# Attention outputs gathered by channel with DMA, and projected without transposes

## The chip, the cores and the metric

The kernel runs on one core of a Trainium2 chip. The metric is device time in microseconds, median of several runs. Engines: PE (TensorE, matrix products), ACT (ScalarE), DVE (VectorE), POOL (GpSimd), and SP (SyncE), whose sequencer here issues every DMA.

## What is computed

```
xn = layernorm(x)                        # x: 8 batches, 1024 tokens, 256 channels, float32
Q, K, V = xn wq^T, xn wk^T, xn wv^T      # 16 heads of 16 channels; rotary embedding on Q and K
attn = softmax(causal(Q K^T / 4)) V      # per head
s = attn wo^T
g = silu(down(silu(gate(xn)) * up(xn)))  # weights are int32, scaled by 1/127
out = x + s * g
```

## The kernel before

It has two phases. `project_phase` writes q, k, v and the gate g to DRAM; `attention_phase` begins at about 400 us. Float32 accuracy is had by splitting operands into a high and a low float16 part.

The attention phase runs over 8 batches of 4 **groups**; a group is four heads of one batch (a `step` is (batch, group)). All engines run the same group loop, each in its own written order, and meet at semaphores.

A group has 36 **turns** on PE, set by the string `ORDER`. An E turn makes one of 18 units of keys-by-queries scores (L1363), from which ACT makes exponentials (`pr`, L1281). An M turn makes one of 18 units of queries-by-keys scores (L794, with the causal mask added by products with `future` and `pick`, L802), of which DVE takes the maximum (L818). These maxima are for later groups: a group takes maxima 7 to 17 of the next group and 0 to 6 of the one after it. Turn t writes two PSUM banks, slot t mod 3, and waits in `wait_slot` until the unit of turn t-3 has been consumed, by ACT if that was an E turn, by DVE if it was an M turn.

Between turns PE runs whole-array blocks at places given by numbers: ten products with v (`times_v`, L1380, `V_AT`; places of 36 and above fall in the next group), a transpose of the joined maxima (L833, `MAXT`), and the work on finished outputs. Product s=0 waits until ACT has copied the second half of the group before out of its bank (`take_output`, L1288, `TAKE1`), product s=3 until it has copied the first half of this group (`TAKE0`).

Outputs of a group come out of `times_v` with channels on partitions: per head 16 rows of output, one row of sums (v is extended with a column of ones, the rest zero) and 15 rows of zeros. ACT copies each half (512 queries) to `ot`, PE transposes it (`transpose_output`, L1394, four 128x128 float32 per half, `OUT1`, `OUT0`), ACT copies it to `on` (L1293), DVE inverts the 16 sums of a row (L1171, `NORM1`, `NORM0`), POOL multiplies into `an` (L1109). When the four groups of a batch are done, its eight tiles of 128 tokens are projected, two in each later group (`output_tiles`): POOL splits a tile (L1099, L1101, `HALVE`), PE transposes the parts (`transpose_tile`, L1402, `TR`), ACT copies them to `aT` (L1298), PE multiplies by wo (`project_tile`, L1410, `WO`), ACT copies the product to `ws` (L1304, `MUL`), POOL multiplies by the gate and adds x (`ADD`). The first batch's four groups have no tiles to project, so no L1402 and no L1410 runs in them. The last group and the four tiles after it have orders of their own (`last_group`, `end_tiles`).

The maxima of the next group are transposed, negated on DVE (L840, `NEG`), split on POOL (L849, L851) and stored by SP as rows of `qs` (`load_max`, L861); the first E turn of the next group waits for that. SP's queue per group is: 8 loads of q and k (L775 to L778), one of v, tile loads and stores in some groups, and the 4 of `load_max`.

## Time and profile before

| | us |
|---|---|
| median of 3 runs | 1221.46 (1220.7 to 1222.96) |
| profiled execution | 1220.83 |
| its span | 1219.1 |

Busy shares of the span: PE 96%, DVE 80%, ACT 72%, POOL 52%. The second phase is a nearly periodic run of groups, each between 24.4 and 25.1 us long, so a change of one group counts some thirty times. A busy time is the union of modelled spans; what an instruction occupies is better read from one start to the next.

### The profile page before, as it was taken

What the parts mean: (1) busy time and instruction counts of PE and PEld (TensorE: products, weight loads), DVE (VectorE), ACT (ScalarE), POOL (GpSimd) and SP (SyncE); (2) the same over time, 40 slices, a digit from 0 to 9 for tenths busy, and PEclk for the clock granted to TensorE, in tenths of its full rate; (3) what the DMA queues carried; (4) which work ended last, traced back from release to release, by engine and by line L of the source; (5) the groups of instructions that cost most, each with busy time, mean ns of one, the idle gap of its engine ahead of it and who ended that gap; (6) DMA issues with size and microseconds to landing.
All of it is one profiled execution on the core that took longest, in us unless ns stands there. A gap on an engine that the chain in (4) does not pass through costs nothing.

```text
span 1219.1 us, 29979 instructions
## 1 busy us (share of the span) xinstructions
PE 1176.2 (96%) x10707; PEld 554.8 (46%) x10707; DVE 971.1 (80%) x1160; ACT 880.6 (72%) x1123; POOL 638.2 (52%) x996
## 2 busy tenths in 40 slices
PE   5999999999999889999999999999999999999997
PEld 3565556656555333334444443444444444444333
DVE  6666666667777689988898899889888988898843
ACT  4554554454444588788888888888888888888884
POOL 5765665765564322444455445554565455445554
PEclk9999999999999899999999999999999999999998
DMA  9755454566642511332323313333144133332122
GB/s 254 191 173 155 141 187 135 157 191 172 167 136 87 147 45 46 98 79 72 97 76 110 97 46 106 73 103 97 49 122 113 45 98 88 97 97 58 59 71 88
DMA packets 157888, 134.81 MB, mean 111 GB/s; under 512 B 49472, under 2 KB 142144, under 8 KB 157760
## 3 DMA queue, kind: packets, MB, share of 16 engines
q1 hardware_dynamic: 157760, 133.08, 38.7%
q8 instruction: 83, 1.36, 0.5%
q14 instruction: 45, 0.37, 0.1%
HBM read 72.61 MB, written 50.33 MB: 101 GB/s over the span
## 4 chain that ended last, share of the span: by engine, by line
PE 61%; ACT 2%; DVE 1%; issue 1%; POOL 1%; ACTq 0%; DVEq 0%; POOLq 0%
PE ps L1380 23%; PE ps L1363 14%; PE ps L794 12%; PE ps L1410 4%; PE ps L802 3%; PE ps L1394 3%; PE ps L1402 2%; ACT pr L1281 1%; DVE mxp L818 1%; PE ps L833 1%; ACT on L1293 0%; POOL ah L1101 0%; POOL zt L1119 0%; DVE yt L1219 0%; ACT ot L1288 0%
## 5 line engine op out<-in xcount | busy, mean ns | idle before, releaser
L818 DVE TENSOR_REDUCE mxp<-ps 128x2 f32<-128x1024 f32 (+2 forms) x576 | 685.3, 1221 | 91.0 <-PE ps L802 50.6
L1281 ACT ACTIVATE pr<-ps 128x1024 f32<-128x1024 f32 x576 | 575.8, 1023 | 100.5 <-PE ps L1363 86.1
L1380 PE MATMUL ps<-pr,vt 128*32 128x512 f32 (+3 forms) x3072 | 315.3, 497 | 0.6 <-POOL pr L1091 0.5
L1363 PE MATMUL ps<-qs,ks 50*128 50x512 f16 (+3 forms) x1536 | 225.6, 329 | 8.6 <-DVE mxp L818 4.2
L794 PE MATMUL ps<-ks,qs 48*128 48x512 f16 (+2 forms) x1792 | 225.2, 304 | 8.2 <-ACT pr L1281 4.8
L1091 POOL TENSOR_SCALAR_AFFINE_SELECT pr<-pr 128x256 f32<-128x256 f32 (+1 forms) x448 | 191.6, 454 | 51.3 <-ACT pr L1281 51.0
L1363 PEld LDWEIGHTS ps<-qs,ks 50*128 50x128 f16 x1536 | 65.4, 93 | 212.7 <-issue 201.6
L674 PE MATMUL ps<-xTh,wguT 128*128 128x512 f16 x384 | 145.8, 380 | 1.2 <-ACT vs L558 1.1
L674 PE MATMUL ps<-xTl,wguT 128*128 128x512 f16 x384 | 145.5, 379 | 0.0
L794 PEld LDWEIGHTS ps<-ks,qs 48*128 48x128 f16 x1792 | 83.0, 94 | 98.6 <-issue 85.0
L849 POOL TENSOR_SCALAR mp<-mneg 32x128 f16<-32x128 f32 x32 | 9.3, 289 | 206.3 <-issue 200.9
L1380 PEld LDWEIGHTS ps<-pr,vt 128*32 128x32 f32 x3072 | 67.3, 108 | 104.4 <-issue 94.7
L433 DVE SCALAR_TENSOR_TENSOR h<-ps,sg 128x512 f32<-128x512 f32 x96 | 65.8, 686 | 48.6 <-ACT sg L566 36.9
L552 ACT ACTIVATE parts<-rr 128x1024 f16<-128x1024 f32 x32 | 33.8, 1057 | 77.8 <-POOL rr L500 77.6
L566 ACT ACTIVATE sg<-ps 128x512 f32<-128x512 f32 x96 | 57.1, 595 | 43.5 <-PE ps L674 23.6
L802 PE MATMUL ps<-future,pick 64*128 64x128 bf16 (+3 forms) x1024 | 85.7, 242 | 0.0
L648 PE MATMUL ps<-xTh,wqkT 128*128 128x512 f16 x256 | 80.4, 384 | 4.4 <-DVE wqkT L383 4.4
L361 POOL TENSOR_TENSOR hl<-h,hh 128x512 f16<-128x512 f32 x64 | 72.8, 1159 | 22.2 <-ACT hh L572 22.2
L424 DVE TENSOR_TENSOR rot<-ps,trig 128x1024 f32<-128x1024 f32 x64 | 75.3, 1219 | 7.5 <-PE ps L648 7.1
L1127 POOL TENSOR_TENSOR yt<-ws,gt 128x256 f32<-128x256 f32 x53 | 38.6, 729 | 76.3 <-ACT ws L1304 76.3
L500 POOL TENSOR_TENSOR rr<-rot 128x1024 f32<-128x1024 f32 x32 | 74.9, 2361 | 5.8 <-DVE rot L424 5.8
L1109 POOL TENSOR_TENSOR an<-on,rec 128x256 f32<-128x256 f32 x61 | 37.9, 622 | 60.6 <-DVE rec L1171 60.6
(104 smaller groups left out, 1355.9 us busy)
## 6 DMA issues: line engine op xcount, KB each, us to landing
v_d<-vs SPq DMA_DIRECT2D x16, 1024.0 KB, 5.3
vt<-v_d SPq DMA_DIRECT2D x32, 512.0 KB, 4.0
xs<-in_L_attn_x SPq DMA_DIRECT2D x16, 512.0 KB, 4.5
q_parts_d<-parts SPq DMA_DIRECT2D x16, 512.0 KB, 3.0
k_parts_d<-parts SPq DMA_DIRECT2D x16, 512.0 KB, 3.1
gate_d<-gs SPq DMA_DIRECT2D x16, 512.0 KB, 3.2
qs<-q_parts_d SPq DMA_DIRECT2D x64, 128.0 KB, 3.1
ks<-k_parts_d SPq DMA_DIRECT2D x64, 128.0 KB, 3.1
```

Source lines behind the costliest of these rows:

```text
L361: eng.tensor_tensor(hl[:, m], h32[:, m % NH], hh[:, m], ALU.subtract).then_inc((lo_pool if m < LOW_POOL else lo_dve).sem, 1)
L424: ins = dve.tensor_tensor(tq[i][:, t], ps[:, (Q0, K0)[i]:(Q0, K0)[i] + 2, :], trig[:, t, :, c * CH:(c + 1) * CH], ALU.mult)
L500: pool.tensor_tensor(rr[i][:, :, :], tq[i][:, :, 0, :], tq[i][:, :, 1, :], ALU.add).then_inc(rot_add.sem, 1)
L648: ins = pe.matmul(ps[:, (Q0, K0)[i] + eo, :], wqkT[:, wp, kd, 2 * i + eo, :], xx[:, c, :, kd, :], start=n == 0, stop=n == len(terms) - 1)
L674: ins = pe.matmul(ps[:, FFN[m] + gu, :], wguT[:, gu, m, kd, :], xx[:, c, :, kd, :], start=n == 0, stop=n == 2 * KD - 1)
L794: ins = pe.matmul(ps[:, slot + t, n * w:(n + 1) * w], qs[r, j, qb * P:(qb + 1) * P], ks[r, j, lo:lo + w], start=n == 0, stop=not any(maske ...
L802: ins = pe.matmul(o, pick[r, half ^ t, :], future[r, half ^ t, 0:len(pieces), half * TILE:P], start=False, stop=half == 1, skip_group_chec ...
L818: dve.tensor_reduce(dst, ps[:, slot:slot + 2, :].rearrange("p t (n s) -> p (t n) s", s=w), axis=AX.X, op=ALU.max).then_inc(keep["max_dve"] ...
L1091: pool.affine_select(out=blk, in_=blk, compare_op=ALU.is_ge, fill=0.0, base=0, pattern=[[0, 2], [0, len(hs)], [1, P]], channel_multiplier= ...
L1281: act.activation(probs(step, s).rearrange("p (t j) s -> p t j s", t=2)[:, :, hs[0]:hs[-1] + 1, 0:w], ps[:, slot:slot + 2, 0:w * len(hs)].r ...
L1363: ins = pe.matmul(ps[:, slot + t, o:o + w], ks[g][r, j, kb * P:(kb + 1) * P], qs[g][r, j, lo:lo + w], start=o == 0, stop=True, skip_group_ ...
L1380: ins = pe.matmul(ps[VW * j:VW * (j + 1), O0, lo - c * CH:CH], vt[g % 2][:, kb, j, :], probs(step, s)[:, j, at:at + w], start=first, stop= ...
```

## The change

The ones now fill columns 16 to 31 of extended v, so that a head's sum comes out on 16 rows beside its 16 output rows. Each half of a group's `ot` is moved by SP with 8 DMAs (`move_output`; 16 partitions of 2 KB each) into `oc` (outputs) and `sc` (sums), which hold 256 channels on partitions. Per tile DVE inverts the sums in `sc` (128x256), POOL multiplies and splits straight into `aT`, and PE projects. Gone are both kinds of transposes, the copies to `on` and `aT`, the small reciprocals and the broadcasting product. The order of turns, the places of the blocks, and the last group's order are new. The maxima's transpose and negation no longer wait for output copies but for the copy of tile 1's product.

```diff
-                            prep(pool.memset(vs[:, :, :, :], 0.0))
-                            prep(pool.memset(vs[:, :, :, DK:DK + 1], 1.0))
+                            prep(pool.memset(vs[:, :, :, :], 1.0))
...
-        ORDER = "EMEMEMEMEMEMEEMEMEMMEMEMEMEMEMEMEMEM"
+        ORDER = "EMEMEMEMMEMEMEMEMEMEMEMEMEMEEMEMEMEM"
...
-            V_AT = (9, 12, 16, 23, 27, 30, 35, TURNS + 1, TURNS + 4, TURNS + 6)
+            V_AT = (7, 10, 13, 22, 27, 30, 33, 35, TURNS + 2, TURNS + 4)
...
-            TAKE1, OUT1, NORM1 = 3, 18, 14
-            TAKE0, OUT0, NORM0 = 8, 21, 14
-            MAXT, NEG, SPLIT_AT = 25, 12, 10
-            HALVE, ADD = (0, 7), (8, 17)
-            COPY, SCALE = (11, 9), (17, 12)
-            TR, EV, WO, MUL = (7, 26), (4, 13), (15, 33), (8, 16)
+            TAKE1, TAKE0, MAXT, NEG, SPLIT_AT = 2, 6, 26, 13, 13
+            INVERT, HALVE, ADD = (0, 5), (5, 9), (12, 13)
+            WO, MUL = (16, 24), (10, 11)
...
+                def move_output(step, c):
+                    b, g = step
+                    if g == 0 and b > 1:
+                        sp.wait_ge(t_lo.sem, t_lo.after((b - 2, (c + 1) * CT - 1)))
+                    sp.wait_ge(o_act.sem, o_act.after(step, c + 1))
+                    for j in range(GH):
+                        r, o = g % 2 * GH * DK + j * DK, j * VW
+                        sp.dma_start(oc[b % 2][r:r + DK, g // 2, c * CH:(c + 1) * CH], ot[o:o + DK, c]).then_inc(o_in[b % 2][c], 16)
+                        sp.dma_start(sc[b % 2][r:r + DK, g // 2, c * CH:(c + 1) * CH], ot[o + DK:o + VW, c]).then_inc(o_in[b % 2][c], 16)
...
                     if prev:
+                        move_output(nth(step, -1), 1)
...
+                    move_output(step, 0)
                     if ahead(step, 1):
                         sp.wait_ge(st_pe.sem, st_pe.after(earlier(nth(step, 1), NG)))
                         load_max(sp, keep, nth(step, 1))
...
+                def scale_tile(tile):
+                    pool.wait_ge(t_rec.sem, t_rec.after(tile))
+                    pool.tensor_tensor(columns(oc, tile), columns(oc, tile), columns(sc, tile), ALU.mult).then_inc(t_norm.sem, 1)
...
+                def invert_sums(tile):
+                    b, t = tile
+                    dve.wait_ge(*landed((b, NG - 1), t // CT))
+                    dve.reciprocal(columns(sc, tile), columns(sc, tile)).then_inc(t_rec.sem, 1)
...
                 def take_output(step, c):
-                    act.wait_ge(o_pe.sem, o_pe.after(earlier(step, 1), c + 1))
+                    if step != (0, 0):
+                        act.wait_ge(*landed(nth(step, -1), c))
...
                         if n == MAXT and ahead(step, 1):
-                            pe.wait_ge(o_copy.sem, o_copy.after(step, 1))
-                            transpose_max(pe, ps, keep, nth(step, 1), M0, D)
+                            if tiles[1]:
+                                pe.wait_ge(t_out.sem, t_out.after(tiles[1]))
+                            pe.wait_ge(mx_neg.sem, mx_neg.after(step))
+                            transpose_max(pe, ps, keep, nth(step, 1), M0)
```

DVE from one negation of maxima to the next, in a group with tiles, before: `mxp` receives a unit's maxima, `mxa` their join, `rec` inverted sums.

```order
L840 TENSOR_SCALAR mneg<-ps 32x128
L818 TENSOR_REDUCE mxp<-ps 128x2 x2
L1171 RECIPROCAL rec<-on 128x16 x2
L818 TENSOR_REDUCE mxp<-ps 128x2 x8
L818 TENSOR_REDUCE mxp<-ps 128x4 x4
L818 TENSOR_REDUCE mxp<-ps 128x8 x2
L827 TENSOR_REDUCE mxa<-mxp 128x32
L818 TENSOR_REDUCE mxp<-ps 128x2 x2
```

The same stretch after; `sc` is inverted in place.

```order
L839 TENSOR_SCALAR mneg<-ps 32x128
L817 TENSOR_REDUCE mxp<-ps 128x2 x5
L1177 RECIPROCAL sc<-sc 128x2x128
L817 TENSOR_REDUCE mxp<-ps 128x2 x4
L817 TENSOR_REDUCE mxp<-ps 128x4
L1177 RECIPROCAL sc<-sc 128x2x128
L817 TENSOR_REDUCE mxp<-ps 128x4 x3
L817 TENSOR_REDUCE mxp<-ps 128x8 x2
L826 TENSOR_REDUCE mxa<-mxp 128x32
L817 TENSOR_REDUCE mxp<-ps 128x2 x3
```

The two 16-element reciprocals stood together behind two maxima; the two of 256 elements now stand behind the first maximum of a group (the last of the x5) and behind the sixth.

PE after, turns 11 to 16 of a group with tiles: L1336 is an E turn, L793 an M turn (L801 its mask), L1353 a product with v, L1361 the projection.

```order
L1336 MATMUL ps<-qs,ks 128x512 x2
L793 MATMUL ps<-ks,qs 128x256 x4
L801 MATMUL ps<-future,pick 128x2x128 x2
L801 MATMUL ps<-future,pick 128x2x64 x2
L1336 MATMUL ps<-qs,ks 128x512 x2
L1353 MATMUL ps<-pr,vt 32x256 x4
L793 MATMUL ps<-ks,qs 128x256 x4
L1336 MATMUL ps<-qs,ks 128x512 x2
L793 MATMUL ps<-ks,qs 128x256 x4
L1361 MATMUL ps<-woT,aT 128x256 x6
```

The piece before with its transposes of outputs, turns 17 to 21 (L1394 reads `ot`).

```order
L1363 MATMUL ps<-qs,ks 128x512 x2
L794 MATMUL ps<-ks,qs 128x256 x4
L1394 MATMUL ps<-ident,ot 128x128 x4
L794 MATMUL ps<-ks,qs 128x128 x8
L802 MATMUL ps<-future,pick 128x512 x2
L802 MATMUL ps<-future,pick 128x4x64 x2
L1363 MATMUL ps<-qs,ks 128x512 x2
L794 MATMUL ps<-ks,qs 128x128 x8
L802 MATMUL ps<-future,pick 128x512 x2
L802 MATMUL ps<-future,pick 128x4x64 x2
L1394 MATMUL ps<-ident,ot 128x128 x4
```

The L1394 blocks and, elsewhere in the group, the two L1402 blocks have no counterpart after; the ten L1353 blocks stay, two of them instead of three at the start of the next group.

## Rows read from the trace of the kernel before

**Rows 1.** Page, part 1: busy us, share, instructions; part 2: granted clock.
```profile
PE 1176.2 (96%) x10707; PEld 554.8 (46%) x10707; DVE 971.1 (80%) x1160; ACT 880.6 (72%) x1123; POOL 638.2 (52%) x996
...
PEclk9999999999999899999999999999999999999998
```

**Rows 2.** One line's instructions (L840), two stretches: duration, first and last start.
```profile
L840 DVE TENSOR_SCALAR mneg<-ps x3: 269/269/269, 460.4 to 509.3; 32x128 f32<-32x128 f32 x3
...
L840 DVE TENSOR_SCALAR mneg<-ps x19: 269/269/271, 705.3 to 1146.7; 32x128 f32<-32x128 f32 x19
```

**Rows 3.** PE, one group without tiles (461.0 to 485.4): busy, mean ns, idle before.
```profile
L1363 PE MATMUL ps<-qs,ks 50*128 50x512 f16 (+3 forms) x48 | 7.0, 327 | 1.0 <-DVE mxp L818 1.0
L794 PE MATMUL ps<-ks,qs 48*128 48x512 f16 (+2 forms) x56 | 7.0, 302 | 1.0 <-ACT pr L1281 0.9
```

**Rows 4.** Timeline of PE: start, us, idle before; blocks and turns of two groups.
```profile
722.40 0.64 PE L1380 MATMUL ps<-pr,vt 128*32 128x256 f32 x8
722.97 0.39 PE L1363 MATMUL ps<-qs,ks 50*128 50x512 f16 x2
723.20 0.38 PE L794 MATMUL ps<-ks,qs 48*128 48x256 f16 x4
723.51 0.66 PE L1394 MATMUL ps<-ident,ot 128*128 128x128 f32 x4
724.10 0.40 PE L794 MATMUL ps<-ks,qs 48*128 48x128 f16 x8
...
726.83 1.06 PE L1380 MATMUL ps<-pr,vt 128*32 128x512 f32 x8
727.83 0.39 PE L1363 MATMUL ps<-qs,ks 50*128 50x512 f16 x2
...
729.18 0.40 PE L1402 MATMUL ps<-identh,ah 128*128 128x128 f16 x4
729.51 0.39 PE L794 MATMUL ps<-ks,qs 48*128 48x512 f16 x2
...
733.82 0.83 PE L1410 MATMUL ps<-woT,aT 128*128 128x256 f16 x6
734.58 0.39 PE L1363 MATMUL ps<-qs,ks 50*128 50x256 f16 x4
```

**Rows 5.** Timeline of PE in groups without tiles: a stall, and turns 0 and 13.
```profile
464.25 0.26 PE L802 MATMUL ps<-future,pick 64*128 64x128 bf16 x4
465.19 0.40 PE L1363 MATMUL ps<-qs,ks 50*128 50x256 f16 x4 [0.67 <-DVE mxp L818]
...
466.73 0.39 PE L1363 MATMUL ps<-qs,ks 50*128 50x512 f16 x2
...
475.47 0.39 PE L1363 MATMUL ps<-qs,ks 50*128 50x512 f16 x2
```

**Rows 6.** Timeline of DVE: maxima, reciprocals, negation.
```profile
463.33 0.35 DVE L1171 RECIPROCAL rec<-on 128x16 f32<-128x16 f32 x2
...
482.56 2.35 DVE L818 TENSOR_REDUCE mxp<-ps 128x2 f32<-128x1024 f32 x2
484.82 0.27 DVE L840 TENSOR_SCALAR mneg<-ps 32x128 f32<-32x128 f32 x1
485.01 1.20 DVE L818 TENSOR_REDUCE mxp<-ps 128x2 f32<-128x1024 f32 x1
```

**Rows 7.** One line's instructions on DVE: ns min/median/max.
```profile
L1171 DVE RECIPROCAL rec<-on x38: 193/218/244, 708.2 to 1149.8; 128x16 f32<-128x16 f32 x38
...
L1182 DVE TENSOR_TENSOR an<-ps,rec x3: 424/424/425, 1184.7 to 1207.3; 128x256 f32<-128x256 f32 x3
```

**Rows 8.** SP: DMA issues of one group, and landing of `qs<-mp`.
```profile
706.10 2.41 SPq L861 DMA_DIRECT2D qs<-mp  x4
710.54 0.33 SPq L775 DMA_DIRECT2D qs<-q_parts_d  x1
710.91 0.42 SPq L776 DMA_DIRECT2D qs<-q_parts_d  x1
...
L861 SPq DMA_DIRECT2D qs<-mp x128: 503/589/1423, 400.5 to 1173.5; - x128
...
DMA to landing us min/median/max: 1.7/1.7/3.0
```

**Rows 9.** The end on PE: last product with v, output and tile transposes.
```profile
1204.81 0.64 PE L1380 MATMUL ps<-pr,vt 128*32 128x256 f32 x8 [0.50 <-POOL pr L1091]
1206.32 0.63 PE L1394 MATMUL ps<-ident,ot 128*128 128x128 f32 x4 [0.87 <-ACT ot L1288]
1208.80 1.30 PE L1402 MATMUL ps<-identh,ah 128*128 128x128 f16 x8 [1.85 <-DVE ah L1230]
```

More of the change, by code:

```diff
@@ L1082, in _ @@
             def _(pool):
[L1083 removed]
+                for s in (causal, t_hi, t_lo, t_norm, t_mul, t_add):
                     s.start(pool)
@@ L1154, in last_group @@
                                 split_tile(tile)
-                            if u == ADD_LAST[i]:
-                                add_gated(tile).then_inc(t_add.sem, 1)
                 over_groups(group, last_group)
-                for i, tile in enumerate(end_tiles):
-                    if i % 2 == 0:
-                        add_gated(tile).then_inc(s_end[0], 1)
+                for tile in end_tiles[1::2]:
+                    pool.wait_ge(t_hi.sem, t_hi.after(earlier(tile, 1)))
+                    pool.wait_ge(t_lo.sem, t_lo.after(earlier(tile, 1)))
+                    split_tile(tile)
@@ L1163, in _ @@
+                for tile in end_tiles[0::2]:
+                    add_gated(tile).then_inc(s_end[0], 1)
             @block.vector
             def _(dve):
-                for s in (o_rec, o_norm):
-                    s.start(dve)
-                def invert_sums(step, c):
-                    dve.wait_ge(o_norm.sem, o_norm.after(earlier(step, 1), c + 1))
-                    dve.wait_ge(o_copy.sem, o_copy.after(step, c + 1))
-                    dve.reciprocal(rec[:, c], on[:, c].rearrange("p (r v) -> p r v", v=VW)[:, :, DK]).then_inc(o_rec.sem, 1)
@@ L1251, in last_group, with sums, result @@
-                    normalise(step, 1)
+                    def sums(i):
+                        invert_sums(last_tiles[i])
+                        scale_tile(last_tiles[i])
+                    def result(i):
+                        gate_product(last_tiles[i], tile_bank(i))
+                        dve.wait_ge(t_add.sem, t_add.after(earlier(last_tiles[i], 1)))
+                        add_gated(last_tiles[i]).then_inc(t_add.sem, 1)
+                    for i in range(3):
+                        sums(i)
@@ L1253, in _ @@
+                    for i in range(3):
+                        result(i)
+                    for i in range(3, len(last_tiles)):
+                        sums(i)
+                    for i in range(3, len(last_tiles)):
+                        result(i)
                 over_groups(group, last_group)
                 for tile in end_tiles:
-                    split_tile(tile)
+                    invert_sums(tile)
+                    scale_tile(tile)
                 for i, tile in enumerate(end_tiles):
-                    b, t = tile
+                    if i % 2 == 0:
+                        dve.wait_ge(t_lo.sem, t_lo.after(earlier(tile, 1)))
+                        low_part(tile)
@@ L1258, in _ @@
+                for i, tile in enumerate(end_tiles):
                     gate_product(tile, i)
                     if i % 2:
[L1260 to L1262 removed]
+                        add_gated(tile).then_inc(s_end[1], 1)
             @block.scalar
             def _(act):
[L1266 removed]
+                for s in (expo, o_act, t_out):
@@ L1310, in group @@
                         for i in range(2):
-                            if u == EV[i] and tiles[i]:
-                                if i == 1:
-                                    act.wait_ge(mx_neg.sem, mx_neg.after(nth(step, 1)))
-                                take_tile(tiles[i], M0)
                             if u == MUL[i] and tiles[i]:
@@ L1336, in _ @@
                 for i, tile in enumerate(end_tiles):
-                    act.wait_ge(t_ev.sem, t_ev.after(earlier(tile, 1)))
-                    take_tile(tile, i)
+                    if i % 2 == 0:
+                        act.wait_ge(t_hi.sem, t_hi.after(earlier(tile, 1)))
+                        act.wait_ge(t_norm.sem, t_norm.after(tile))
+                        act.wait_ge(t_wo.sem, t_wo.after(earlier(tile, TILES)))
+                        act.activation(aT[:, tile[1] % TILES, 0], columns(oc, tile), ACT.Copy).then_inc(t_hi.sem, 1)
             @block.tensor
             def _(pe):
-                for s in (st_pe, pv_pe, o_pe, t_tr, t_wo):
+                for s in (st_pe, pv_pe, t_wo):
                     s.start(pe)
```

192 lines of the change are left out of this document (46 added, 146 removed).

## The prediction

> **What bounds the kernel now.** I read the page first: PE is busy 96% at nearly full granted clock, DVE 80% [rows 1]. That invites the sum "take work off PE, gain that time". The second view contradicts it. A group's period is the distance between two negations: (509.3 - 460.4)/2 = 24.45 us in the first batch, (1146.7 - 705.3)/18 = 24.52 us later [rows 2]. The first batch's groups run no tile transposes and no projections. From start to start a projection occupies 0.76 us (733.82 to 734.58), a tile transpose 0.33, and the unit ahead of a whole-array block occupies 0.31 instead of 0.22 [rows 4]. So those groups have 2 x 0.76 + 2 x 0.33 + 4 x 0.09 = 2.5 us less PE work, and are only 0.07 us shorter. The difference turns up as waits: PE stands about 1.0 us for DVE's maxima and 1.0 us for ACT's exponentials per group [rows 3], one of them 0.67 us on a single maximum [rows 5]. What bounds a group is the hand-over of three slots among PE, DVE and ACT: the turn three places later waits for the consumer. PE work inside such a wait is free, and so is its removal.
>
> **What PE loses.** An output transpose occupies 0.59 us (723.51 to 724.10), a tile transpose 0.33 [rows 4]. Per group 2 x 0.59 + 2 x 0.33 + 4 x 0.09 = 2.2 us go. PE's own floor falls from 24.5 to 22.3 us. ACT loses four copies of about 0.6 us each and is no bound (72%). POOL trades one product for another of 128x256.
>
> **What DVE gains.** Before, the two reciprocals of 16 elements stand 0.16 us apart and the second lasts 0.19 [rows 6, 7]. After, there are two of 256 elements, R us each. This is the unknown, and it decides. A maximum occupies 1.13 us (2.35 less 1.22 for two) for 1024 elements, the negation 0.19 (484.82 to 485.01) for 128 [rows 6]: about 1.04 ns per element and 0.06 fixed. Lower bound: the reciprocal streams the same way, 256 x 1.04 + 60 = 330 ns, and with what its 16-element form costs beyond such streaming once (about 80 ns for the first of a pair, 0.16 - 0.08), R = 0.41. Upper bound: the whole 160 ns of the first, less 60, is per element: 6.2 ns, R = 1.65. Between them stands the second of a pair. Its duration is 50 ns below the first's (193 against 244), so it occupies some 110 ns; less 60 that is 3.2 ns per element, R = 0.06 + 0.82 + 0.05 for a first = 0.93. I take 0.93, because in this reading the overhead is that of every other DVE row and only the per-element cost is special; the lower bound needs a fixed extra that no other row shows.
>
> The Trainium skill, page "VectorE: DVE Perf Modes", section "Walkthrough: the 8-slice pipeline in each mode", says that reciprocal runs as a hardware iterative divide with a repeat count of 8. Read as eight cycles per element, an estimate from that page's clock gives R = 2.2 and a time near 1313. The trace does not bear that reading out: sixteen elements would take 133 ns beyond the fixed part, and the second of a pair has no room for that. It supports more than one cycle per element.
>
> **The walk through a group.** I follow the 36 turns with the rows' durations: E 0.22 (0.31 with a 384-wide piece), M 0.22 to 0.66 by mask, a v product 1.00 or 0.57, maxima 1.13 each, exponentials 0.92; a consumer sees PE's result 0.2 to 0.27 us after it and PE a release 0.14 after an end. Turn t waits for the unit of t-3. The walk of the kernel before gives 24.63 for the 24.52 of the rows, and 24.52 without tiles for 24.45, with the stalls where the trace has them; its turn 13 starts 8.71 after turn 0, the trace says 475.47 - 466.73 = 8.74 [rows 5].
>
> After, the group falls into two parts. **Head, turns 0 to 15.** DVE starts the group's first maximum 0.66 us after turn 0 and from then on is never idle: seven maxima (turns 1, 3, 5, 7, 8, 10, 12) and both reciprocals come before the release that the E of turn 15 waits for. 0.66 + 7 x 1.13 + 2R + 0.22 = 8.8 + 2R. PE's own work there is some 8.5 us, so with R above 0.3 DVE decides, and each reciprocal's time is added to the period twice over, once per tile. **Rest, turns 15 to 35.** PE decides: 11 E 2.65, 10 M 3.44, five v products 5.0 (one more than before, which is taken out of the next head), two projections 1.52, the maxima's transpose 0.3, entries to 8 blocks 0.76, sum 13.7; waits for slots left at turns 18 to 21, for tile 1's product at turn 26 and small ones 1.1. Together 14.8. Period: 23.6 + 2R for large R; for R below 0.4 the walk stays at 24.48, since PE and the exponentials then close the head. R = 0.93 gives 25.49, which is 0.86 above the walk of before; R = 0.41 gives 24.49, 0.14 below; R = 1.65 gives 26.93, 2.3 above. Even R = 0 would not give the 22.3 of PE's floor.
>
> **Groups of the first batch** have no reciprocal: 24.26 against 24.52, four groups, -1.0 us. **27 groups with tiles:** 27 x 0.86 = +23.2.
>
> **SP and the moves.** 16 DMAs per group are added to SP's queue, ahead of `load_max`. Bounds for an issue: 0.42 us (q and k loads) and 0.59 (`qs<-mp`) [rows 8]. In the walk the second eight are issued from 10.4 us, after ACT's copy, and done at 14 to 15.5; the maxima's parts are ready at 19.7. Behind them wait `load_max` and through it the next group's first turn: parts 19.7 + 4 x 0.6 + 1.7 landing = 23.8, before 25.5. I cost the moves at nothing; the cover is 4 us on the queue and 1.7 us at the end. ACT's wait for a landed move is a group old.
>
> **Last group and end.** The last group loses seven tile transposes (7 x 0.42), two output transposes and one leftover v product, 5.5 us of PE, but its fourth projection now waits for copy, eight issues (3.4 to 4.7), landing 1.7, inversion, product and split: I count -4 us, between -6 and 0. At the end, the last v product to the span's end was 1219.1 - 1205.4 = 13.7 us [rows 9]. After: copy 0.6, issues 3.4 to 4.7, landing 1.7, four tiles on DVE at R + 0.5 (a product is 0.42 [rows 7]), then some 7 for split, projection, gate, store: 18.5 to 20, +5. Together +1; for R = 0.41 -2, for R = 1.65 +4.
>
> **Sum.** Span 1219.1 - 1.0 + 23.2 + 1 = 1242.3; outside the span 1.7 us as in the profiled run: 1244. The profiled execution lies 0.6 below the median, so 1244 holds for the median as well.
>
> **Rivals.**
> - *The reciprocal is cheap* (R about 0.4): 27 x -0.14 - 1.0 - 2 = -7, giving 1214. For it: every other DVE row streams at one element per 1.04 ns. Against it: the 50 ns of the second of a pair beyond that. This ends on the other side; it decides from R below about 0.45, and up to 0.55 the result is within 0.2%. Chance 0.27.
> - *The reciprocal costs what the first of a pair shows* (R about 1.65): 27 x 2.3 - 1 + 4 = +65, giving 1286. Chance 0.17.
> - *R near 0.5 to 0.7*: +2 to +10, 1222 to 1231. Chance 0.06.
> - *PE's work is the bound after all* and the turns adapt: 27 x -2.2 - 4 x 1.3 = -65, giving 1156. Against it speak [rows 2, 3]: 2.5 us less PE work made a group 0.07 shorter. Chance 0.04.
> - *Moves hold up `load_max`*: SP's first eight moves start 4.2 us into the group, the load of v and eight more follow, and `load_max` must start by 21.4. So 4.6 + 16 issues has to stay under 21.4: it decides from 1.05 us per issue, and each further 0.1 us costs 1.6 us a group. The longest `qs<-mp` issue took 1.42 [rows 8], the typical ones half of that. At 1.15 it adds 50 us, giving about 1294. Chance 0.04.
>
> The forecast has the remaining 0.42.
>
> **How the numbers follow.** What a measurement of this kernel can tell from no change is about 0.2%, 2.4 us. Faster by more: the cheap reciprocal less what of it ends near zero, 0.24, and PE's floor 0.04: 0.28. Within: 0.09. Slower: 0.42 + 0.17 + 0.04: 0.63. The range reaches from the cheap to the dear reciprocal with their spreads, 1209 to 1287; it leaves out PE's floor, the slow queue and the outer edges, under 0.2. The forecast's own range is 1232 to 1254.
>
> **What would show it.** Right: L1177 lasts about 1.0 us; negations 25.3 us apart with tiles and 24.2 in the first batch; PE's idle time before E turns goes to DVE's maxima, mostly at turns 6 and 15; DVE above 90% busy; no wait for `mp` or `qs` at turn 0. Wrong: L1177 at 0.4 us or at 1.7; a period in the first batch well below 24.2, which would mean that the slots do not bound; idle PE at the first turn of groups, which would put it on SP.

## The result

| | median us | runs | profiled span us | mean granted clock |
|---|---|---|---|---|
| before | 1222.21 (1220.7 to 1224.21) | 4 | 1219.1 | 0.99 |
| after | 1309.27 (1308.02 to 1311.3) | 4 | 1307.2 | 0.96 |

The ratio is 1.0718, with an interval of 1.0703 to 1.0733. The direction was forecast, the size was not: 1244 was predicted, and 1287 was the upper end of the range.

### The profile page after: what moved, and what is told of

Its sections match the earlier page's. It is cut to its first block, busy times and chain, and to the rows that moved or that the text cites. A ratio compares the mean times of both kernels' runs of the same rounds, so it can differ in the third digit from the quotient of the medians.

```text
span 1307.2 us, 29048 instructions
## 1 busy us (share of the span) xinstructions
PE 1160.6 (89%) x10195; PEld 521.1 (40%) x10195; DVE 1060.1 (81%) x1162; ACT 823.1 (63%) x1007; POOL 641.2 (49%) x984
## 4 chain that ended last, share of the span: by engine, by line
PE 38%; DVE 24%; ACT 2%; issue 2%; SPq 1%; DMA 1%; POOL 0%; ACTq 0%; DVEq 0%; POOLq 0%
DVE mxp L817 16%; PE ps L1353 14%; PE ps L1336 9%; PE ps L793 8%; DVE sc L1177 7%; PE ps L1361 4%; ACT pr L1269 2%; PE ps L801 2%; PE ps L832 1%; SPq L1060 1%; SPq L1061 0%; DMA sc<-ot 0%; DMA qs<-mp 0%; DVE oc L1196 0%; SPq L860 0%
## 5 line engine op out<-in xcount | busy, mean ns | idle before, releaser
L817 DVE TENSOR_REDUCE mxp<-ps 128x2 f32<-128x1024 f32 (+2 forms) x576 | 676.6, 1215 | 94.3 <-PE ps L801 57.5
L1353 PE MATMUL ps<-pr,vt 128*32 128x512 f32 (+3 forms) x3072 | 326.4, 513 | 1.2 <-ACT ot L1277 1.0
L1336 PE MATMUL ps<-qs,ks 50*128 50x512 f16 (+3 forms) x1536 | 232.5, 338 | 88.5 <-DVE mxp L817 80.6
L1109 POOL TENSOR_SCALAR_AFFINE_SELECT pr<-pr 128x256 f32<-128x256 f32 (+1 forms) x448 | 194.6, 451 | 214.7 <-ACT pr L1269 214.5
L793 PE MATMUL ps<-ks,qs 48*128 48x512 f16 (+2 forms) x1792 | 236.8, 317 | 14.2 <-ACT pr L1269 7.4
L1336 PEld LDWEIGHTS ps<-qs,ks 50*128 50x128 f16 x1536 | 71.1, 95 | 282.0 <-issue 278.5
L793 PEld LDWEIGHTS ps<-ks,qs 48*128 48x128 f16 x1792 | 83.7, 97 | 163.8 <-issue 154.7
L1177 DVE RECIPROCAL sc<-sc 128x256 f32<-128x256 f32 x64 | 111.5, 1743 | 15.7 <-DMA sc<-ot 15.7
L1353 PEld LDWEIGHTS ps<-pr,vt 128*32 128x32 f32 x3072 | 67.6, 109 | 101.6 <-issue 75.1
L801 PE MATMUL ps<-future,pick 64*128 64x128 bf16 (+3 forms) x1024 | 92.8, 256 | 0.0
L565 ACT ACTIVATE sg<-ps 128x512 f32<-128x512 f32 x96 | 57.1, 595 | 43.6 <-PE ps L673 23.6
L551 ACT ACTIVATE parts<-rr 128x1024 f16<-128x1024 f32 x32 | 33.8, 1057 | 77.7 <-POOL rr L500 77.5
L1361 PE MATMUL ps<-woT,aT 128*128 128x256 f16 x384 | 55.0, 283 | 23.5 <-DVE aT L1218 16.4
```

What stands on the lines that cost most here:

```text
L793: ins = pe.matmul(ps[:, slot + t, n * w:(n + 1) * w], qs[r, j, qb * P:(qb + 1) * P], ks[r, j, lo:lo + w], start=n == 0, stop=not any(maske ...
L801: ins = pe.matmul(o, pick[r, half ^ t, :], future[r, half ^ t, 0:len(pieces), half * TILE:P], start=False, stop=half == 1, skip_group_chec ...
L817: dve.tensor_reduce(dst, ps[:, slot:slot + 2, :].rearrange("p t (n s) -> p (t n) s", s=w), axis=AX.X, op=ALU.max).then_inc(keep["max_dve"] ...
L1109: pool.affine_select(out=blk, in_=blk, compare_op=ALU.is_ge, fill=0.0, base=0, pattern=[[0, 2], [0, len(hs)], [1, P]], channel_multiplier= ...
L1177: dve.reciprocal(columns(sc, tile), columns(sc, tile)).then_inc(t_rec.sem, 1)
L1336: ins = pe.matmul(ps[:, slot + t, o:o + w], ks[g][r, j, kb * P:(kb + 1) * P], qs[g][r, j, lo:lo + w], start=o == 0, stop=True, skip_group_ ...
```

## The profile after

The page of the kernel after, its busy time and its granted clock (as [rows 1]):

```profile
PE 1160.6 (89%) x10195; PEld 521.1 (40%) x10195; DVE 1060.1 (81%) x1162; ACT 823.1 (63%) x1007; POOL 641.2 (49%) x984
...
PEclk9999999999998999899989999899989999989986
```

PE has fallen from 96% to 89%. Its clock, full everywhere between the first phase and the end before, now shows dips all through the attention phase.

The negations of maxima mark the groups (L839 here, L840 in [rows 2]): their count, then ns, then the first and last start. First the groups without tiles, then those with tiles.

```profile
L839 DVE TENSOR_SCALAR mneg<-ps x3: 269/269/269, 458.2 to 506.7; 32x128 f32<-32x128 f32 x3
...
L839 DVE TENSOR_SCALAR mneg<-ps x25: 268/269/271, 560.5 to 1216.7; 32x128 f32<-32x128 f32 x25
```

Without tiles: (506.7 - 458.2)/2 = 24.25 us a group, against 24.45 before. With tiles: (1216.7 - 560.5)/24 = 27.34, against 24.52. So the loss is in the groups that project tiles, as forecast, but it is 2.8 us each instead of 0.86.

The new reciprocal, all of its instructions in those groups (ns min/median/max), and one of them on DVE's timeline (start, us):

```profile
L1177 DVE RECIPROCAL sc<-sc x51: 1741/1743/1744, 520.6 to 1205.1; 128x256 f32<-128x256 f32 x51
...
568.27 1.74 DVE L1177 RECIPROCAL sc<-sc 128x256 f32<-128x256 f32 x1
569.93 1.16 DVE L817 TENSOR_REDUCE mxp<-ps 128x2 f32<-128x1024 f32 x1
```

From start to start it occupies 569.93 - 568.27 = 1.66 us. That is R, taken as 0.93 and bounded by 1.65 above.

PE at the same place, and 7 us later; the bracket is the idle time ahead of the row and what ended it:

```profile
569.41 0.39 PE L793 MATMUL ps<-ks,qs 48*128 48x512 f16 x2
571.24 0.40 PE L1336 MATMUL ps<-qs,ks 50*128 50x384 f16 x4 [1.45 <-DVE mxp L817]
...
576.66 0.39 PE L793 MATMUL ps<-ks,qs 48*128 48x256 f16 x4
578.50 0.39 PE L1336 MATMUL ps<-qs,ks 50*128 50x512 f16 x2 [1.44 <-DVE mxp L817]
```

These are the E turns 6 and 15. Two such waits stand in each group with tiles but the first, which has only one reciprocal and one wait; one stands behind each reciprocal, and the second is 1.0 to 1.2 us long where the clock has just been lowered. They are PE's waits on DVE between 560 and 1216 us (in total, times, longest):

```profile
PE ps L1336 <- DVE mxp L817: 66.9, 49, 1.5
```

Then the clock. Each row below is one group of the kernel after (length, busy time of each engine, granted clock, DMA share, GB/s):

```profile
675.70:704.40 28.70, 25.72 (x250) 9.53 (x246) 24.70 (x23) 19.57 (x22) 13.08 (x26) 0.88 0.27 66
731.90:758.50 26.60, 23.13 (x252) 9.00 (x248) 24.50 (x23) 19.57 (x22) 13.12 (x26) 1.00 0.32 79
...
839.30:867.00 27.70, 24.43 (x252) 9.26 (x248) 24.59 (x23) 19.58 (x22) 13.09 (x26) 0.94 0.35 88
```

The same instructions take 26.6 us at full clock, 27.7 at 0.94 and 28.7 at 0.88. Inside the slow stretch of the first of them PE works at the lower level:

```profile
693.30 0.61 PE L1336 MATMUL ps<-qs,ks 50*128 50x512 f16 x2
693.68 0.66 PE L793 MATMUL ps<-ks,qs 48*128 48x512 f16 x2
...
695.26 0.39 PE L1336 MATMUL ps<-qs,ks 50*128 50x512 f16 x2
695.49 0.38 PE L793 MATMUL ps<-ks,qs 48*128 48x512 f16 x2
```

0.61 and 0.66 us for what takes 0.39 and 0.38 two microseconds later: 1.2 GHz, then 2.4 GHz. Of the 27 groups with tiles ten take 26.6 us, the last one 25.7, and the others 27.3 to 28.8. The first of the 27 takes 27.3, with one reciprocal and a fall of the clock.

The end, DVE first, then two of the eight moves on SP, then PE's wait:

```profile
1289.81 1.75 DVE L1177 RECIPROCAL sc<-sc 128x256 f32<-128x256 f32 x1 [7.52 <-DMA sc<-ot]
1291.66 0.42 DVE L1196 TENSOR_TENSOR oc<-oc,sc 128x256 f32<-128x256 f32 x1
1292.01 1.74 DVE L1177 RECIPROCAL sc<-sc 128x256 f32<-128x256 f32 x1
...
1283.46 0.51 SPq L1060 DMA_DIRECT2D oc<-ot  x1
1284.01 0.59 SPq L1061 DMA_DIRECT2D sc<-ot  x1
...
1299.15 3.09 PE L1361 MATMUL ps<-woT,aT 128*128 128x256 f16 x15 [16.45 <-DVE aT L1218]
```

**Where the 88.1 us of span went.** Counted from the first E turn of each group in both traces (PE's start at L1363 and L1336): up to the first group 415.7 -> 414.2 (-1.5); the four groups of the first batch 99.9 -> 98.4 (-1.5); the 27 groups with tiles 660.0 -> 735.7 (+75.6); the last group up to its last product with v 29.1 -> 33.8 (+4.7); from there to the end 14.3 -> 25.1 (+10.8).

## The experiments

The theory to be tested: in each group the slots hand the lead to DVE in the head, so each reciprocal's time goes into the period in full, twice, and the division alone makes the loss. The rivals: PE's work bounds; the moves by DMA cost something; the order itself is worse. A second question came from the trace: why the clock falls.

**1. The changed kernel without a division.** The results are left undivided.

```diff
-                    dve.reciprocal(columns(sc, tile), columns(sc, tile)).then_inc(t_rec.sem, 1)
+                    dve.tensor_tensor(columns(sc, tile), columns(sc, tile), columns(sc, tile), ALU.subtract).then_inc(t_rec.sem, 1)
```

> The kernel after, with each 128x256 reciprocal replaced by a subtraction of the same size in the same place (sums become zero, so the attention part of the output is left out). Nothing else moves. Slot theory (the hand-over of three slots bounds a group, and each reciprocal adds its occupancy R to every group twice): with about 0.33 us in place of 1.66 the negations are 24.1 to 24.4 us apart in groups with tiles (27.3 on the mean in the kernel after), 24.2 in the first batch, and the time is about 1220 us: 1219.1 span before - 3.5 for 27 groups - 3 for the first batch + 6 for a longer end. PE-floor theory (PE's own work bounds a group once the reciprocal is cheap): 22.3 us per group, about 1165 us. Moves theory (the DMA moves and SP's queue cost something by themselves): above 24.6 us per group, above 1228 us. Granted clock: back near 0.99 if PE's long waits lowered it, still 0.96 if the moves did.

Measured: 1231.3 (1229.49 to 1232.43), ratio 1.0073 (1.0053 to 1.0093).

```profile
L839 DVE TENSOR_SCALAR mneg<-ps x24: 269/269/269, 581.9 to 1147.5; 32x128 f32<-32x128 f32 x24
...
560.00:1150.00 590.00, 555.35 (x5904) 215.73 (x5898) 539.90 (x528) 469.98 (x529) 316.30 (x625) 1.00 0.43 108
```

A group takes (1147.5 - 581.9)/23 = 24.59 us and the clock is full again (1.00). 78 of the 87 us are gone. The subtraction was not as cheap as I had assumed: it occupies 0.52 and 0.68 us from start to start in a group, not 0.33, which may be why the group is 0.1 above the walk. Two things follow. The rival of PE's floor (1165) is refuted. And with a subtraction in place of the division the rest of the change still isn't faster than before: the groups stand at 24.6 against 24.5, and the last group and the end take 51.9 us instead of 43.4 from the last group's first E turn on. The total lies where I had written "the moves cost something by themselves" (above 1228), and 24.59 is just under the 24.6 of that case. Most of the 10 us above the kernel before is 8.5 in the last group and the end, where the moves stand in series with the rest. What the groups would take with nothing in the division's place wasn't tested.

**2. Half the size.** Each reciprocal runs over 64 of its tile's 128 tokens, and the products read those twice, so the results of the other tokens are not the reference's.

```diff
-                    dve.reciprocal(columns(sc, tile), columns(sc, tile)).then_inc(t_rec.sem, 1)
+                    dve.reciprocal(columns(sc, tile)[:, :, 0:P // 2], columns(sc, tile)[:, :, 0:P // 2]).then_inc(t_rec.sem, 1)
```

> The kernel after, with each reciprocal over the first 64 tokens of a tile only (128x128 elements), used for both halves of the tile (the normalisation of the other 64 tokens is wrong by that). Price per element, from 1.66 us for 256 elements: a reciprocal occupies 0.86 us. Slot theory with 2R per group: negations 25.0 us apart in undisturbed groups (26.6 - 1.6), and about 1240 us in all. If the reciprocal has a large fixed part, R stays above 1.2 and the groups above 25.6. PE-floor theory: DVE's 20.9 + 1.7 us of work leave it below PE, so 22.6 us per group and about 1175 us.

Measured: 1244.3 (1243.25 to 1245.68), ratio 1.0184 (1.0166 to 1.0202).

```profile
L1178 DVE RECIPROCAL sc<-sc x48: 941/943/944, 565.2 to 1146.6; 128x128 f32<-128x128 f32 x48
...
L839 DVE TENSOR_SCALAR mneg<-ps x23: 269/269/271, 582.5 to 1132.4; 32x128 f32<-32x128 f32 x23
```

A reciprocal of 128x128 lasts 0.943 us instead of 1.743, 0.80 less; a group takes (1132.4 - 582.5)/22 = 25.00 instead of 26.59, 1.59 less. That is twice 0.80: the full time, once per tile, as the walk said.

**3. The other way round: the kernel before plus two reciprocals.** They run on a buffer that nobody else reads, behind the first and the sixth maximum of a group, in 26 of the 27 groups with tiles (the first of them gets none).

```diff
+                dve.memset(idle[:, :], 1.0).then_inc(s_idle, 1)
+                dve.wait_ge(s_idle, 1)
...
+                        if n in (0, 5) and output_tiles(step)[0]:
+                            dve.reciprocal(idle[:, :], idle[:, :]).then_inc(s_idle, 1)
```

> The kernel before, with two reciprocals of 128x256 on a buffer of their own, in DVE's order behind the first and the sixth maximum of every group with tiles: the cost of the division alone, with all transposes kept and no moves. Slot theory, walked through the old order: 26.3 us per group against 24.6 in the same walk without them, so +1.7 in each of 27 groups, +45 us, 1267 us; with a lowered clock after PE's waits up to 1285 us. PE-floor theory: PE's 24.5 us and DVE's 24.3 us of work both fit in nearly the old period, under +10 us, below 1232 us.

Measured: 1262.09 (1260.15 to 1263.52), ratio 1.0325 (1.0303 to 1.0346).

```profile
L840 DVE TENSOR_SCALAR mneg<-ps x22: 268/269/270, 585.6 to 1134.3; 32x128 f32<-32x128 f32 x22
...
560.00:1150.00 590.00, 556.50 (x5918) 228.32 (x5914) 559.56 (x542) 486.64 (x588) 291.64 (x596) 1.00 0.30 83
```

(1134.3 - 585.6)/21 = 26.13 us a group. Nothing was moved, no order was changed, and nearly half of the loss is there (41 of 87 us). That only 1.6 of the 3.3 us of added DVE work count fits the slack that DVE had in the old order: its idle time per group falls from 2.6 to 1.3 us (busy 528 and 560 of 590 us). The other 47 us are not in this kernel: groups of 26.6 instead of 26.1 at full clock (12), the lowered clock (18) and the longer last group and end (16).

**4. The kernel before with fewer transposes.** In all but the last group and the end, one transpose of four is left in each block; the copies read it four times. The results are not the reference's. The diff shows PE's side; the copies' new reads are not shown.

```diff
-                    for a in range(CT):
+                    for a in range(1 if freed is o_copy else CT):
...
-                    for lo in range(2):
-                        for kd in range(KD):
+                    few = tile not in last_tiles + end_tiles
+                    for lo in range(1 if few else 2):
+                        for kd in range(1 if few else KD):
```

> The kernel before, with one transpose in place of four in each output block and each tile block outside the last group, and the copies behind them reading that one block four times (their size and the order of everything stay; most of the attention output is wrong). PE loses about 2 x 0.44 + 2 x 0.24 = 1.4 us per group. Slot theory: 0.2 us per group with tiles and 0.15 in the first batch at most come back, 1215 to 1218 us. PE-floor theory: -1.4 x 27 - 0.9 x 4 = -41 us, 1180 us.

Measured: 1218.83 (1218.04 to 1219.79), ratio 0.9973 (0.9962 to 0.9983).

```profile
L840 DVE TENSOR_SCALAR mneg<-ps x24: 268/268/270, 583.4 to 1146.8; 32x128 f32<-32x128 f32 x24
```

(1146.8 - 583.4)/23 = 24.50 against 24.52, and 1218.8 in all, just above the 1215 to 1218 that I had written. Three quarters of the transposes are gone from these groups, but not three quarters of their time: a block of one output transpose still occupies 0.37 us instead of 0.59, and one of a tile as much as the block of four. The busy times of the same stretch, the kernel before and then this one:

```profile
560.00:1150.00 590.00, 588.69 (x6308) 244.84 (x6306) 528.05 (x531) 518.18 (x626) 305.35 (x624) 1.00 0.31 87
560.00:1150.00 590.00, 572.92 (x6030) 224.33 (x6028) 527.43 (x532) 516.91 (x627) 304.61 (x625) 1.00 0.32 86
```

PE's busy time falls by 15.8 us in 24 groups, 0.66 a group and not the 1.4 of my expectation, and its idle time grows by the same amount. So 0.66 us of PE work a group was free. The first row says something else that a learner should see: in groups with tiles PE of the kernel before stood still for only 1.3 of 590 us. It was full, and yet it was not the bound, because the hand-over of the slots takes just as long.

**5. The price of a division by its size.** The kernel before, with reciprocals in one uninterrupted series on DVE in the last group, and two products behind them.

```diff
+                for n, w in enumerate((16, 16, 16, 32, 32, 64, 64, 128, 128, 256, 256, 512)):
+                    dve.reciprocal(dst[:, n * 512:n * 512 + w], src[:, 0:w]).then_inc(s_idle, 1)
+                for n, w in enumerate((256, 256), 12):
+                    dve.tensor_tensor(dst[:, n * 512:n * 512 + w], src[:, 0:w], src[:, 0:w], ALU.mult).then_inc(s_idle, 1)
```

> The kernel before, with reciprocals of one operand at the end of VectorE's last group, one behind the other with nothing between: 128x16 three times, 128x32 twice, 128x64 twice, 128x128 twice, 128x256 twice, 128x512, and then two 128x256 products. It prices the division by its size. Reading of the first of a pair in the trace before (6.2 ns an element): start to start 0.13, 0.23, 0.43, 0.83, 1.65 us for 16, 32, 64, 128, 256. Reading of the second of a pair (3.2 ns), on which the prediction stood: 0.08, 0.14, 0.25, 0.45, 0.93. The changed kernel's own 1.66 us says the first; if so, the short second ones of a pair in the trace before were no measure of the work, and the 128x16 ones here should show how a second one of equal size is recorded.

There is one execution (1232.17 us), and only its rows are used. The groups of that stretch by form (count, then busy us and mean ns), and two rows of its timeline, the first with both of 256, the second with the last of 256 and the one of 512:

```profile
L1260 DVE RECIPROCAL dst<-src 128x256 f32<-128x256 f32 x2 | 3.3, 1694 | 0.0
L1260 DVE RECIPROCAL dst<-src 128x512 f32<-128x512 f32 x1 | 3.3, 3295 | 0.0
L1260 DVE RECIPROCAL dst<-src 128x128 f32<-128x128 f32 x2 | 1.7, 895 | 0.0
L1260 DVE RECIPROCAL dst<-src 128x64 f32<-128x64 f32 x2 | 0.9, 494 | 0.0
...
L1260 DVE RECIPROCAL dst<-src 128x32 f32<-128x32 f32 x2 | 0.5, 295 | 0.0
L1260 DVE RECIPROCAL dst<-src 128x16 f32<-128x16 f32 x3 | 0.5, 211 | 0.0
...
1212.20 3.31 DVE L1260 RECIPROCAL dst<-src 128x256 f32<-128x256 f32 x2
...
1213.81 4.91 DVE L1260 RECIPROCAL dst<-src 128x256 f32<-128x256 f32 x2
...
1218.63 0.69 DVE L1262 TENSOR_TENSOR dst<-src 128x256 f32<-128x256 f32 x2
```

Per element: (3295 - 1694)/256 = 6.25 ns, (1694 - 895)/128 = 6.24, (494 - 295)/32 = 6.2. Start to start: 1213.81 - 1212.20 = 1.61 us for 256 elements, 0.41 for 64, 0.21 for 32, and 0.11 for the second 128x16. So a reciprocal in a series occupies 6.25 ns times its elements and some 10 ns, and one that follows another kind of instruction some 50 ns more. The two products of 256 elements start 0.28 us apart, which leaves about 10 ns beside the 1.05 ns per element of the maxima. The fixed part was never the 60 ns that the prediction subtracted.

**6 and 7. Work in PE's waits.** Nine matmuls whose result nobody uses ahead of two E units, in 26 of the 27 groups with tiles (not in the first). In the first of the two kernels I put the second block one E unit too late (unit 8 instead of 7).

```diff
+                        if n in (E_TURN[3], E_TURN[7]) and tiles[0]:
+                            pe.wait_ge(mx_neg.sem, mx_neg.after(step))
+                            for _ in range(9):
+                                pe.matmul(ps[:, M0, 0:D], woT[:, 0, 0, 0:P], woT[:, 0, 0, :], start=True, stop=True)
```

> The changed kernel with nine 128x256 matmuls (fp16, result unused) ahead of the two E units in each group with output tiles at which TensorE stood 1.44 us for VectorE's maximum. They should fit into those waits (nine of 0.11 to 0.12 us, 1.0 to 1.1). Theory one, the waits on VectorE lower TensorE's granted clock, and the lowered clock makes some groups 27.3 to 28.7 us long instead of 26.59: every group at 26.59, granted clock near 1.00, 27 groups 718 instead of 735.7, total about 1291. Rival, the lowered clock has to do with the moves or with the divisions and not with TensorE's standing: 1309, with the granted clock at 0.96 as before. Rival, the added matmuls delay the E units: above 1309 with all groups alike and longer than 26.59.

Measured with unit 8: 1322.29 (1320.97 to 1325.35), ratio 1.0835 (1.0807 to 1.0862). Most groups take 27.57 us, 0.98 more, since the misplaced block stood on the path. Only three of the 27 groups are longer than 27.8, which already speaks for the theory on the clock, but the period had changed too. (The edit shown is that of the second kernel.)

> The sixth experiment with its second block of nine matmuls moved from E unit 8 to E unit 7 (turn 15): the trace of the changed kernel shows the waits of 1.44 us ahead of units 3 and 7, and ahead of unit 8 the block cost the path 0.98 us a group (27.57 instead of 26.59). Now both blocks lie in waits. Theory one (waiting on VectorE lowers TensorE's granted clock): nearly every group with tiles at 26.59, clock 0.99 or more, 27 groups 718 to 724 instead of 735.7, total 1292 to 1298. Rival (the lowered clock comes from something else): 27 groups at 735 and 1309, clock 0.96.

Measured with unit 7: 1290.12 (1288.5 to 1291.11), ratio 1.0555 (1.0537 to 1.0573).

```profile
569.80 1.16 PE L1372 MATMUL ps<-woT 128*128 128x256 f16 x9
571.32 0.40 PE L1336 MATMUL ps<-qs,ks 50*128 50x384 f16 x4 [0.36 <-DVE mxp L817]
...
L839 DVE TENSOR_SCALAR mneg<-ps x23: 268/269/269, 560.6 to 1145.8; 32x128 f32<-32x128 f32 x23
...
560.00:1216.00 656.00, 624.93 (x6521) 260.82 (x6520) 603.48 (x542) 482.17 (x542) 324.88 (x645) 1.00 0.39 98
```

The block fills the wait, the E turn starts where DVE lets it, and the clock stays full: (1145.8 - 560.6)/22 = 26.60 us a group, 27 groups in 717.5 us instead of 735.7. 468 useless matmuls make the kernel 19 us faster, 2 us below the 1292 to 1298 that I had written. The one group without a block, the first with tiles, is the control: its wait stays, and the clock falls as it ends (the second row lasts 0.66 us, and 0.40 at full clock).

```profile
523.64 0.45 PE L1336 MATMUL ps<-qs,ks 50*128 50x512 f16 x2 [1.44 <-DVE mxp L817]
523.85 0.66 PE L793 MATMUL ps<-ks,qs 48*128 48x256 f16 x4
```

So the lowered clock was the second part of the loss, and PE's waits caused it; the reciprocals and the moves are the same in both kernels.

**8. Lowered clock without moves.** The third experiment with 384 elements instead of 256.

```diff
-        idle = sb("idle", [P, D], F32)
+        idle = sb("idle", [P, 3 * D // 2], F32)
```

> The kernel before, with two reciprocals of 128x384 each on VectorE in the head of each group with output tiles, where the third experiment had two of 128x256 (26.11 us a group, 1262). No moves, no change to the order. Slot theory: each occupies 384 x 6.2 ns plus a little = 2.45 us, 0.8 more, so a group takes 26.11 + 1.6 = 27.7 us where the clock is full: 1262 + 27 x 1.6 = 1305. If TensorE's standing lowers its clock, then here too, though nothing is moved by DMA: granted clock near 0.96 in the tile groups and 15 to 30 us on top, 1320 to 1335. If the moves lowered it: clock 0.99 and 1305.

Measured: 1343.44 (1342.21 to 1344.7), ratio 1.0996 (1.0971 to 1.1021).

```profile
631.50:661.90 30.40, 27.44 (x266) 10.43 (x262) 26.44 (x25) 21.80 (x26) 12.71 (x26) 0.89 0.23 62
...
775.80:803.50 27.70, 24.63 (x268) 10.14 (x264) 26.39 (x25) 21.59 (x26) 12.72 (x26) 1.00 0.32 87
```

Groups at full clock take 27.7, as forecast (26.1 + 2 x 0.8). The clock falls in others, and more than I allowed for: the total is 8 us above the upper end of what I wrote. Since this kernel moves no outputs, the moves are not needed for it. PE's longest wait on DVE between 560 and 1150 us is 1.8 us here, and the group above has 0.89; in the third experiment it is 1.0 us, and the clock is 1.00.

The length of the longest wait does not decide alone. The traces of experiments 1, 2 and 10 each have one group of the first batch that takes 25.4 us instead of 24.2, with a clock of 0.93. There is no division in these groups, and ahead of the fall the longest wait in the group is 0.5 us. In experiment 1 (the group, then a row that takes 0.51 us at full clock):

```profile
462.80:487.00 24.20, 22.14 (x228) 7.53 (x220) 20.57 (x21) 17.88 (x20) 6.04 (x14) 0.93 0.33 78
...
477.53 0.88 PE L801 MATMUL ps<-future,pick 64*128 64x512 bf16 x4
```

Why one of four equal groups is hit, and in three of the kernels only, stays open.

**9. The moves twice.** The kernel of the first experiment, with each half copied once more to a buffer in DRAM.

```diff
+                    for j in range(GH if step != LAST else 0):
+                        sp.dma_start(dup_d[b, g, c, j, 0], ot[j * VW:j * VW + DK, c]).then_inc(o_in[b % 2][c], 16)
+                        sp.dma_start(dup_d[b, g, c, j, 1], ot[j * VW + DK:(j + 1) * VW, c]).then_inc(o_in[b % 2][c], 16)
```

> The first experiment's kernel (the changed one, with a subtraction in place of each division; 1231.3, 24.58 us a group) in which each half of the outputs is also copied a second time, to a scratch buffer in DRAM: sixteen issues on SP instead of eight. SP stood idle for some 6.4 us of a 24.58 us group, and the added issues take 16 x 0.6 = 9.6, so SP's queue should become the bound: 24.58 - 6.4 + 9.6 = 27.8 a group and about 1231 + 30 x 3.2 = 1327, with TensorE waiting on qs<-mp. Rival, issues on SP are free here: 1231. In between (the cover of 1 to 4 us ahead of the load of the maxima alone counts): 1245 to 1270.

Measured: 1391.24 (1390.19 to 1396.93), ratio 1.1388 (1.1361 to 1.1415). PE's waits between 560 and 1150 us, and below it the same line of the kernel after over its whole span (who waited for `qs<-mp`):

```profile
PE ps L1340 <- DMA qs<-mp: 77.3, 19, 6.1
```

```profile
L860 SPq DMA_DIRECT2D qs<-mp x128: 503/589/1337, 399.3 to 1244.8; - x128
...
  PE ps L1336: 0.6, 1
```

With sixteen more issues a group, SP is the bound and PE stands up to 6.1 us at a group's first turn. Groups take 27.2 to 32.7 us, 30.1 on the mean, where I had 27.8, and the total is 64 us above my 1327. The sum of SP's issues left out what it waits for in between (40 us for ACT's copies between 560 and 1150 us), and the clock of this stretch is 0.92; the shares weren't separated. In the kernel after, PE waited once in the whole run for `qs<-mp`, 0.6 us. So the eight moves per half are hidden in the groups, by a cover that one more such set uses up.

**10. The end from two queues.** The kernel after, with four of the last eight moves issued by ScalarE.

```diff
-                    for j in range(GH):
+                    for j in range(GH) if (step, c) != (LAST, 1) else (0, 2):
...
+                for j in (1, 3):
+                    r, o = g % 2 * GH * DK + j * DK, j * VW
+                    act.dma_start(oc[b % 2][r:r + DK, g // 2, CH:2 * CH], ot[o:o + DK, 1]).then_inc(o_in[b % 2][1], 16)
+                    act.dma_start(sc[b % 2][r:r + DK, g // 2, CH:2 * CH], ot[o + DK:o + VW, 1]).then_inc(o_in[b % 2][1], 16)
```

> The changed kernel, with the eight moves of the very last half issued from two queues, four by SP and four by ScalarE, which has nothing to do then. The eight issues took 4.9 us in series on SP, with VectorE's last four reciprocals and all of the end behind them. If the end hangs on the series of issues: 4 x 0.6 = 2.4 us less, about 1306.9, and VectorE's idle time ahead of the first of the last four reciprocals 7.5 -> 5.1. If it hangs on the landing: no change, 1309.3.

Measured: 1306.64 (1304.03 to 1310.03), ratio 1.0696 (1.0663 to 1.073). The interval overlaps that of the kernel after, so the total alone is inconclusive. The row decides:

```profile
1289.07 1.75 DVE L1177 RECIPROCAL sc<-sc 128x256 f32<-128x256 f32 x1 [5.63 <-DMA sc<-ot]
```

DVE's idle time ahead of the first of the last four reciprocals is 5.63 instead of 7.52. Four issues on ScalarE took 0.60 to 0.78 us each, so it was 1.9 instead of the 2.4 expected.

## Why the prediction was wrong

**What bounds the kernel: right.** The slots, not PE's work: experiment 4 takes work off PE in the kernel before, experiment 1 takes the dear division out of the changed kernel, which has less PE work, and neither gives a group clearly shorter than before. The groups without tiles came out at 24.25 against 24.26 predicted.

**What PE loses: worth nothing, as predicted.** Its size, 2.2 us a group, wasn't confirmed: PE's busy time per group with tiles is 24.5 us before (588.69/590 x 24.52) and 23.1 in experiment 1 (555.35/590 x 24.59), 1.3 less. Busy times are unions of modelled spans, so they don't settle it.

**What DVE gains: this is the step that failed.** R was put at 0.93 us and measured 1.66; L1177 lasts 1.743, which is the prediction's own sign of being wrong ("at 1.7"). The row itself was read well. "The second of a pair" occupied some 110 ns; experiment 5 has 0.11 for it too. The error was in the next clause, "less 60 that is 3.2 ns per element". The 60 ns came from maxima and a negation that read PSUM, and were carried over to a reciprocal that reads SBUF right behind another. There the fixed part is about 10 ns, so the 110 ns were nearly all division: 100/16 = 6.25 ns. (The 3.2 ns were rounded up as well: 50/16 is 3.1.) The 50 ns by which the first of a pair is longer were fixed, and those I had counted as work in the upper bound, which thereby came out right by accident: its 160 - 60 leaves the same 100 ns. The argument for the middle value, that "the overhead is that of every other DVE row", was the unproven assumption.

Of the page "VectorE: DVE Perf Modes" of the Trainium skill (section "Walkthrough: the 8-slice pipeline in each mode") the prediction had said that the trace speaks against reading its repeat count of 8 as eight cycles per element. It does: by an estimate from the clock of 0.96 GHz on that page, the measured 6.25 ns are 6.0 cycles. But the direction in which that page pointed, a division of several cycles per element, was right, and I had given it too little weight. That the time of this reading, 1313, lies near the 1309 measured is chance: by the prediction's own formula R = 2.2 gives 28.0 us a group and some 1316, and what was measured is 26.59 a group and a lowered clock.

**The walk and its formula: the slope right, the level 0.35 us too high.** Period = 23.6 + 2R was forecast. Measured at full clock: 26.59 for R = 1.66 and 25.00 for R 0.80 lower. The slope is 2.0, and the level 26.59 - 3.32 = 23.3. With the right R the prediction's own sum would have been 26.93 and 1286; the measured period at full clock is 26.59. In the difference to the kernel before little of this is left, since the walk gave that one 24.63 for 24.45, also too high.

**A term that was missing: the clock.** 27 x 26.59 = 717.9, experiment 7 has 717.5, and the 27 groups took 735.7. These 18 us are neither in the sum nor among the rivals. PE's idle time was treated as free because it isn't on the path; in experiment 7 filling it gave 19 us.

So the 75.6 us of the 27 groups are 27 x (26.59 - 24.45) = 57.8 of longer groups at full clock and 17.8 of lowered clock. With a subtraction in the division's place the same groups are 2.8 us above before (experiment 1: 662.8 against 660.0), so about 55 of the 57.8 are the divisions'.

**First batch: right** (-1.5 against -1.0).

**The moves cost nothing: right** in the groups, as far as PE's waits show; it waited 0.6 us in total for what they might have held up.

**Last group and end: mis-sized**, +15.5 against +1. The last group was forecast 4 shorter and became 4.7 longer: its fourth projection waited for tile work that itself waited for moves and reciprocals, and PE came out of that wait at the lower clock (1.44 us for six matmuls instead of 0.83):

```profile
1271.68 1.44 PE L1361 MATMUL ps<-woT,aT 128*128 128x256 f16 x6 [6.96 <-POOL aT L1122]
...
1278.93 0.83 PE L1361 MATMUL ps<-woT,aT 128*128 128x256 f16 x6
```

The end was forecast +5 and is +10.8; four reciprocals at 1.66 instead of 0.93 are 2.9 of the missing 5.8. Without a division the two parts together are still 8.5 above before (experiment 1), so about 7 of the 15.5 are the reciprocals' and 8.5 the rest of the change, which I put down to the serial chain of copy, eight issues, landing and tiles. How much of that 8.5 belongs to the last group and how much to the end wasn't separated.

**The rivals.** The dear reciprocal, at 0.17, was the case that came true, at 1286; with groups 2.14 longer instead of 2.3 (-4), the clock (+18), the larger last group and end (+12) and the start up to the first group (-2) it becomes 1310, and 1309 was measured. The cheap reciprocal (0.27) had for it only that other DVE operations stream at 1.04 ns, which says nothing of a division. PE's floor and the slow queue didn't come: the groups are far from 22.3 us, and PE waited 0.6 us for the queue in the whole run. That the measured time lies above even the dear reciprocal's is due to the clock, which no rival had.

**No version beats the kernel before.** Even with a subtraction in place of the division the changed kernel stands 0.7% behind. Of all kernels with the reference's results the one before is the fastest.

## What to carry to other kernels

Price an operation by its size only from rows that differ in size: two lengths of the same instruction give a slope, while one length less an overhead borrowed from other instructions gives a guess. Replicating a small operand so that a later step gets simpler (here the sums, 16 times) is dear when the operation on it is a slow one: 32 elements per partition and group became 512. A full engine is not by that the bound: here TensorE was 99.8% busy in the groups with tiles, and work taken off it came back as waiting. And where an edit turns a full TensorE into one that waits a little in every round, keep a term for its clock.

## What the runs showed of the hardware

- A float32 reciprocal on VectorE takes 6.25 ns per element of a partition, from 16 to 512 elements (experiment 5), about six times a product's 1.05. In a series about 10 ns come on top.
- TensorE's clock fell from 2.4 to 1.2 GHz for stretches between 560 and 1150 us in kernels whose longest waits there were 1.45 us and more (the kernel after, experiments 6 and 8 to 10), and stayed at 1.00 where the longest was 0.4, 0.6, 0.7 or 1.0 (experiments 7, 1, 2 and 3). It also fell once in the first batch behind a wait of 0.5 (experiments 1, 2 and 10). Groups with identical instructions took 26.59 us at full clock or up to 28.8. Filling the waits brought 1.00 back. The Trainium skill's page "TensorE: Matmul & The Clock Gate", section "A second HAM failure mode: psum-queue depth-cycling", tells of a kernel in which frequent short idle times between groups of matmuls made the clock swing between its levels; the trace agrees, with two waits of 1.45 us a group and a granted clock of 0.88 to 0.94 in the groups that were hit. Why some of the equal groups are spared wasn't tested.
- A float32 subtraction of 128x256 that occupies 0.33 us in the first group with tiles (at 522 us) occupies 0.52 and 0.68 by turns in the later ones (experiment 1, start to start). What it meets there wasn't tested.
